# A first attention laid in written orders with its value product in two halves, and last sums moved into the last layer bodies

## The reference

```
xn  = layernorm(x)
out = x + attention(xn) + ffn(xn)
```

## Time and profile before

| | us |
|---|---|
| median of 3 runs | 3527.9 (3526.22 to 3528.53) |
| the profiled execution, whole | 3527.28 |
| its span, first to last instruction | 3525.5 |
| PE busy, share | 3293.5, 93% |
| DVE busy, share | 2843.1, 81% |
| ACT busy, share | 1832.3, 52% |
| POOL busy, share | 2640.0, 75% |

### The profile page before, as it was taken

One profiled execution on the slowest core, in us unless ns is written; L12 is line 12 of the kernel. 1 busy time (PEld: TensorE's weight loads), 2 busy tenths in 40 slices (PEclk: granted clock), 3 DMA queues, 4 the chain that ended last, 5 costly groups with the idle time before them and its releaser, 6 DMA issues. The chain is left out here.

```text
span 3525.5 us, 69882 instructions
## 1 busy us (share of the span) xinstructions
PE 3293.5 (93%) x26940; PEld 1611.1 (46%) x26940; DVE 2843.1 (81%) x3289; ACT 1832.3 (52%) x2692; POOL 2640.0 (75%) x1918
## 2 busy tenths in 40 slices
PE   5788876899999999999999999999999999999986
PEld 3222222454555545454545455555555454545443
DVE  5788846888888888888888888888888888888862
ACT  2477772454545454555555555555454545455532
POOL 3133206998888888888888888888888888888850
PEclk7799998999999999999999999999999999999998
DMA  6232214333333323333323333333333233333211
GB/s 209 73 63 48 47 37 113 79 73 73 71 86 79 80 71 72 83 71 82 78 71 79 79 81 77 73 73 85 83 74 79 68 78 78 83 77 71 71 46 49
DMA packets 178233, 270.01 MB, mean 77 GB/s; under 512 B 42481, under 2 KB 67185, under 8 KB 176241
## 3 DMA queue, kind: packets, MB, share of 16 engines
q1 hardware_dynamic: 174160, 251.10, 29.6%
q10 hardware_dynamic: 3744, 14.43, 1.1%
HBM read 44.49 MB, written 19.55 MB: 18 GB/s over the span
## 5 line engine op out<-in xcount | busy, mean ns | idle before, releaser
L1084 DVE SCALAR_TENSOR_TENSOR ly_prod<-ly_pj_ps,ly_few,ly_tables 128x1024 f32<-128x1024 f32 x768 | 964.6, 1272 | 190.1 <-ACT ly_sq L1216 165.5
L1216 ACT ACTIVATE ly_sq<-ly_pj_ps 128x512 f32<-128x512 f32 x768 | 451.0, 601 | 745.8 <-PE ly_pj_ps L918 702.7
L918 PE MATMUL ly_pj_ps<-ly_xs,ly_wqk 128*128 128x512 f32 x1536 | 796.1, 616 | 35.2 <-DVE ly_prod L1084 22.5
L999 PE MATMUL ly_to_ps<-ly_u,ly_mvo 128*128 128x512 f32 x1536 | 720.6, 598 | 0.1
L1325 POOL TENSOR_TENSOR ly_sq<-ly_sq 128x512 f32<-128x512 f32 x384 | 491.6, 1280 | 220.0 <-ACT ly_sq L1216 219.8
L1247 ACT COPY ly_u<-ly_pair_ps 128x1024 f32<-128x1024 f32 x384 | 378.7, 1013 | 240.6 <-PE ly_pair_ps L987 240.6
L1329 POOL TENSOR_TENSOR ly_sx<-ly_sx,ly_smax 128x1024 f32<-128x1024 f32 x192 | 366.2, 1907 | 145.3 <-DVE ly_smax L1124 145.3
L918 PEld LDWEIGHTS ly_pj_ps<-ly_xs,ly_wqk 128*128 128x128 f32 x1536 | 269.2, 191 | 426.4 <-issue 291.5
L999 PEld LDWEIGHTS ly_to_ps<-ly_u,ly_mvo 128*128 128x128 f32 x1536 | 277.1, 190 | 287.2 <-issue 287.2
L987 PE MATMUL ly_pair_ps<-ly_pt,ly_xt 32*128 32x512 f32 x3072 | 385.3, 615 | 19.9 <-ACT ly_u L1247 13.0
L967 PE MATMUL ly_pair_ps<-ly_kbd,ly_qp 128*32 128x128 f32 x12288 | 374.7, 276 | 22.2 <-DMA ly_kbd<-ly_kr 18.9
(11 more groups left out here) (113 smaller groups left out, 4317.5 us busy)
## 6 DMA issues: line engine op xcount, KB each, us to landing
ly_qp<-ly_qr SPq DMA_DIRECT2D x768, 128.0 KB, 2.3
ly_kbd<-ly_kr SPq DMA_DIRECT2D x1536, 64.0 KB, 2.0
ga_parts_dram<-ga_parts SPq DMA_DIRECT2D x16, 384.0 KB, 2.3
ga_qs<-ga_parts_dram SPq DMA_DIRECT2D x96, 64.0 KB
ga_ks<-ga_parts_dram SPq DMA_DIRECT2D x96, 64.0 KB
ly_wqk<-in_wqk SPq DMA_DIRECT2D x24, 256.0 KB, 4.0
ly_mvo<-mvo_dram SPq DMA_DIRECT2D x6, 1024.0 KB, 6.4
mvo_dram<-ga_pt ACTq DMA_DIRECT2D x4, 1024.0 KB, 4.0
```

The costliest lines, as they stand in the source:

```text
L918: pe.matmul(pj_ps[:, j % 2, :], wqk[:, g, j % TILES, :], xs[:, n % 2, WIN:], start=True, stop=True).then_inc(proj_ready.sem, 1)
L999: last = pe.matmul(to_ps[:], mvo[:, h, :], u[:, :, :, h, :].rearrange("p t c q -> p (t c) q"), start=(h == 0), stop=(h == LH - 1))
L1084: dve.scalar_tensor_tensor(prod[:, k], pj_ps[:, j % 2, :].unsqueeze(1).to_broadcast([P, 2, N]), gains[:, n // B, k:k + 1], tables[:, table ...
L1216: act.activation(sq[:, k, :], pj_ps[:, j % 2, :], ACT.Square).then_inc(sq_done.sem, 1)
```

## The change

- **Attention, orders.** The loops over quads are replaced by one written order per engine (`body(x_0, x_1, x_2, x_3)`, batches i, i-1, i-2, i-3). Score pairs are numbered 0 to 31 (`second(n, i)`), first pairs and maxima likewise. The first score pair of a batch and the first three exponentials are issued at the end of the body before, the last maximum and last product in the body after. `project` is issued by tile, four a batch.
- **Value product.** `pv` becomes `meet(n, q, half)`: 256 columns at a time, placed separately in the order. The same number of columns in all, twice the matmuls.
- **Folds.** A fold has four steps instead of three parts. Layers 0 to 3 write `s_ps` instead of `f_ps`, wait for `early_taken`, and have two buffers in `pt` in turn, `folded_1` and `gained` of their own. Layers 0 and 1 and most of layer 2 are folded in body 0, the rest of 2 and layer 3 in body 1. The tokens of batches 1 to 7 are turned together (`turn_others`) after step 9. Layer 4 begins in bodies 8 and 9; its last two steps and all of layer 5 (steps 18 to 23) are in body 10, behind the last product. The first exponential waits for the stores of layers 2 and 3.
- **SP's order.** Key parts are sent after the maxima of the batch before and stacked last.
- **End.** `final_part` is gone. `load_sums` loads the sums into `wqk` and `tables` when they are free; `turn_back` transposes X into `pj_ps`, for batches 0 and 1 at the end of body 51, 2 to 6 in body 52, 7 after it; `add_sums` adds into the same buffers and `store` writes them out.

The core of the diff:

```diff
-            def pv(b, q):
+            def meet(n, q, half):
...
+                lo = N // 2 * half
                 for c in range(4):
-                    last = pe.matmul(pv_ps[32 * c:32 * c + 32, :], va[:, b % 3, kt, 4 * j + c, :], pt[:, (QUADS * b + q) % 3, c, :],
-                                     start=(kt == 0), stop=(kt == T - 1), skip_group_check=True)
-                last.then_inc(pv_done.sem, 1)
+                    last = pe.matmul(pv_ps[32 * c:32 * c + 32, lo:lo + N // 2], va[:, n % 3, kt, 4 * j + c, :], pt[:, (QUADS * n + q) % 3, c, lo:lo + N // 2],
+                                     start=(kt == 0 and half == 0), stop=(kt == T - 1), skip_group_check=True)
+                if half:
+                    last.then_inc(pv_done.sem, 1)
...
+            def body(x_0, x_1, x_2, x_3):
+                project(x_0, 0); project(x_0, 1); second(x_2, 1); first(x_2, 31); meet(x_3, 15, 0); first(x_1, 0); second(x_2, 2)
+                meet(x_3, 15, 1); fold(x_3, 18); transposed_maxima(x_2, 1); second(x_2, 3); meet(x_2, 0, 0); fold(x_1, 11)
+                first(x_1, 1); project(x_0, 2); project(x_0, 3); second(x_2, 4); first(x_1, 2); fold(x_1, 12); meet(x_2, 0, 1)
+                fold(x_0, 0); out(x_3, 3); fold(x_3, 19); fold(x_3, 20); fold(x_3, 21); fold(x_3, 22); fold(x_3, 23); second(x_2, 5)
+                fold(x_0, 1); first(x_1, 3); second(x_2, 6); first(x_1, 4); meet(x_2, 1, 0); second(x_2, 7); values(x_0)
+                first(x_1, 5); meet(x_2, 1, 1); second(x_2, 8); first(x_1, 6); meet(x_2, 2, 0); second(x_2, 9); fold(x_0, 2)
...
+                first(x_1, 18); meet(x_2, 8, 1); transposed_maxima(x_1, 0); second(x_2, 21); fold(x_0, 8); first(x_1, 19)
+                fold(x_0, 9); turn_others(x_0); meet(x_2, 9, 0); second(x_2, 22); fold(x_0, 10); first(x_1, 20); meet(x_2, 9, 1)
...
+                first(x_1, 25); fold(x_2, 17); second(x_2, 28); first(x_1, 26); meet(x_2, 12, 0); meet(x_2, 12, 1); second(x_2, 29)
+                fold(x_1, 15); first(x_1, 27); meet(x_2, 13, 0); fold(x_1, 16); meet(x_2, 13, 1); second(x_2, 30); first(x_1, 28)
+                meet(x_2, 14, 0); second(x_2, 31); first(x_1, 29); meet(x_2, 14, 1); out(x_2, 2); second(x_1, 0); first(x_1, 30)
...
+            def body(x_0, x_1, x_2, x_3):     # ACT
+                exponentials(x_2, 3, 4); take(x_3, 3); exponentials(x_2, 5, 6, 7, 8, 9, 10, 11, 12, 13, 14, 15); gain_early(x_0, 0)
+                take_early(x_0, 0); take_early(x_0, 1); take_early(x_0, 2); gain_early(x_0, 1); pass_on(x_0, 0); take_early(x_0, 3)
+                take_early(x_0, 4); take_early(x_0, 5); take_early(x_0, 6); copy_values(x_0)
+                exponentials(x_2, 16, 17, 18, 19, 20, 21); pass_on(x_0, 1); take(x_2, 0)
...
+                take_early(x_0, 7); exponentials(x_2, 40); gain_early(x_0, 2); exponentials(x_2, 41, 42, 43, 44, 45, 46, 47)
+                copy_others(x_0); exponentials(x_2, 48); take_early(x_1, 11); exponentials(x_2, 49); take_early(x_0, 8)
...
+            def body(x_0, x_1, x_2, x_3):     # SP
+                send_maxima(x_2, 1); take_maxima(x_2, 1); send_parts(x_0, 0); stack(x_0, 0); send_maxima(x_1, 0); send_parts(x_0, 1)
+                take_maxima(x_1, 0); stack(x_0, 1); store_sum(x_2); store_late(x_2, 0); store_late(x_2, 1)
...
+            def turn_back(*items):
+                for b in items:
...
+                    if b >= 2:
+                        pe.wait_ge(res_done, b - 1)
+                    pe.wait_ge(x2_done.sem, x2_done.at(LAST + b, 1))
+                    for t in range(T):
+                        last = pe.transpose(pj_ps[:, b % 2, t * P:(t + 1) * P], X[:, b, 1 + t * P:1 + (t + 1) * P], ident[:])
+                    last.then_inc(res_ready, 1)
...
+            def add_sums(*items):
+                for b in items:
+                    dve.wait_ge(res_ready, b + 1)
+                    dve.wait_ge(sums_in[b // half], 16)
+                    dve.tensor_tensor(sums(b), pj_ps[:, b % 2, :], sums(b), ALU.add).then_inc(res_done, 1)
```

More of the change, by code:

```diff
@@ L87 @@
 GROUPS_LN = ((0, 1), (1, 4), (4, 8))
[L88 to L92, removed]
+OTHERS = range(1, B)
+EARLY = 4
 def global_attention_part(nc, x_dram, w_dram, rope_dram, ident_dram, X, sum_dram, parts_dram, maxes_dram, d):
@@ L189, in global_attention_part, with bodies, folds, fold_views @@
         where = {}
[L191 to L195, removed]
+        def bodies(body):
+            for i in range(B + 3):
+                body(*(known(i - k) for k in range(4)))
+        def folds(n, layer):
+            return n == (0 if layer < EARLY else B - 1)
+        def fold_views(layer, part):
+            k, f = layer % 2, s_ps[:, 0:2] if layer < EARLY else f_ps[:, where["fold", layer, part]]
             if part < 2:
-                return (folded_vo[late].rearrange("p (j h z c) -> p j z h c", j=2, z=2, c=P)[:, part],
-                        f_ps[:, k].rearrange("p z (h c) -> p z h c", c=P))
-            return folded_1[late], f_ps[:, k].rearrange("p z n -> p (z n)")[:, 0:F1]
+                return (folded_vo[layer].rearrange("p (j h z c) -> p j z h c", j=2, z=2, c=P)[:, part], f.rearrange("p z (h c) -> p z h c", c=P))
+            return folded_1[:, k], f.rearrange("p z n -> p (z n)")[:, 0:F1]
         @block.sync
@@ L361, in fold @@
                     pe.wait_ge(raw_loaded[k].sem, raw_loaded[k].at(layer // 2, 48))
-                to = slot(("fold", layer, part), taken, taken.at(at, part + 1))
+                if layer >= EARLY and part < 3:
+                    slot(("fold", layer, kind), late_taken, late_taken.at(layer - EARLY, kind + 1))
+                elif part < 3 and i:
+                    pe.wait_ge(early_taken.sem, 3 * layer + part)
+                f = s_ps[:, 0:2] if layer < EARLY else f_ps[:, where["fold", layer, kind]]
@@ L418, in _ @@
+            bodies(body)
         @block.vector
@@ L629, in _, with exponentials @@
-            stages(body)
+            def exponentials(n, *heads):
+                if n is None:
+                    return
+                for at in heads:
+                    quad = QUADS * n + at // 4
+                    if n == 0 and at == 0:
+                        for k in range(2):
+                            act.wait_ge(early_stored[k].sem, early_stored[k].at(EARLY // 2 - 1, 32))
+                    if quad >= 3 and at % 4 == 0:
+                        act.wait_ge(pv_done.sem, quad - 2)
+                    act.wait_ge(s_ready.sem, s_ready.at(n, at + 1))
+                    act.activation(pt[:, quad % 3, at % 4, :], s_ps[:, (64 * n + at) % 3, :], ACT.Exp, scale=float(GD) ** -0.5).then_inc(exp_done.sem, 1)
@@ L811, in layers_part @@
         where = {}
+        LAST = ITEMS - B
+        half = B // 2
+        sums = lambda b: wqk[:, b].rearrange("p t c -> p (t c)") if b < half else tables[:, b - half]
         def bodies(body):
@@ L884, in _ @@
             bodies(body)
+            load_sums()
+            for b in range(B):
+                store(b)
+            sp.wait_ge(res_stored, 16 * B)
         @block.tensor
```

607 lines of the change are left out of this document (286 added, 321 removed).

## The result

The changed kernel takes 3469.3 us (median of 4 runs, 3465.5 to 3471.9) against 3527.1 beside it: ratio 0.9834, interval 0.9821 to 0.9847. The profiled execution took 3465.5, its span 3463.4. I forecast 3460, within 3440 to 3487: the profiled execution is 5 us over it, the median 9.

The account below looks back on a forecast made before the run. No engine was full before, PE and ACT waiting in turn; after the change DVE was to bound steady bodies. Terms for bodies, tail and end sum to -67.2 us: 3527.3 to 3460 us, range 3440 to 3487.

Parts of the forecast that it names:

- The mechanism: Steady attention stages: PE and ACT wait for each other in turn, 2.67 us a quad; half products between score pairs end it.
- DVE sets the pace inside: Steady bodies: one more pair of maxima costs DVE 1.14 us, ACT 1.08, PE 1.04; DVE's sum is 41.5 us.
- 41.1 us: PE's summed work in a steady body: score pairs, products, shape switches, projections, output transposes, values and turned maxima.
- 60 cycles a matmul: Overhead rule weighed against halves: 3.2 us more PE a body, body near 47.5; the forecast took no such cost.
- Bodies 3 to 7, 8: Steady attention bodies 3 to 7: 44.3 us each, -35.9 together; body 8, without projections and values: 40.0 us, -6.2.
- Body 2: Attention body 2: 44.3 steady, plus 2.8 for low clock, plus 2.0 for a late store: 49.1 us, -5.2.
- Body 0: Start of the attention: token copies wait behind ACT's DMA issues; body 1 begins at about 59.6 us, -2.5.
- Body 1: Attention body 1: folds grow from 9.7 to 13 us of PE, partly hidden by maxima: change 0, from -4 to +4.
- Body 9, tail: Body 9, bounded by ACT alone: 36.5 us, -8.6; tail from last exponential to layers: 18.3 for 12.0, +6.3.
- End: Final part after the layers: 8.0 us for 23.1, -15.1, bounds -17 to -12.
- The last item's chain: Last layer bodies: turn_back(2) stands ahead of up(0) on PE and waits for add_sums(0), adding 1.4 us.
- SP's queue keeps its time: Attention: key parts go out behind the maxima, some 27 us into a body; 12 loads issued by about 38 of 44.

Follow-up runs that it names:

- the fillers' run: The changed kernel with one more unused 256-column matmul behind each of the 32 first score pairs of batch 0: 3468.7 us, ratio 0.9838.
- the folds moved: The changed kernel with fold steps 17 to 23 moved from behind the last exponential into the body of batch 7's exponentials: 3473.4 us, ratio 0.9848.

## Why the prediction was right or wrong

**The mechanism: right.** I said that PE and ACT wait for each other because 1.00 us of product stands ahead of the next scores, and that halves between pairs end it. Halves alone take the steady body from 51.5 to 47.5.

**"DVE sets the pace inside": wrong.** This is the step that failed, with the sum under it, "41.1 us" for PE, which is busy for 44.0. Taken from start to next start in the same body, the 22 halves that stand alone cost 0.57 each and the ten that stand in five adjacent pairs 1.00 a pair, 17.5 us where I had 16.0. The other terms are each within 0.6, and the sum comes to 42.6. Eight waits behind score pairs add the tails that busy time counts, 1.3, and 2.2 us of idle make the 46.0 up to 0.1. So the sum was 1.5 too low, in the term "16 products at 1.00 = 16". My sums had DVE ahead by only 0.4 (41.5 to 41.1), so that was enough to name the wrong engine.

The extra of the halves was undersized too: I had 1.6 us for the changes between shapes and nothing for the halves themselves, and the work rises by an estimated 2.8 from whole to half products in the same order. The earlier trace rows had a hint, PE busy 43.0 in the stage of before, above DVE's 42.6 and above my sum for more work, though a part of the 43.0 is tails ahead of waits. I built the sum from single rows and did not hold it against the busy time of the same stage.

By the Trainium skill's 60 cycles a matmul (TensorEngine Tiling, Instruction Overhead) the 128 added matmul records should have cost an estimated 3.2 us and the body 47.5. The runs show some 2.8 and 46.0, near the rule in sum but not in its form: two adjacent halves, 16 records, take the same 1.00 us as one whole product of 8, and the extra is at the halves that stand alone between score pairs. The rule did point to the right engine.

**Bodies 3 to 7, 8:** 46.4 us on average for 44.3, and 44.7 for 40.0. Body 8 repeats the error: I gave DVE's 38.9 plus a little, and it has 41.6 of DVE and 41.1 of PE.

**Body 2:** forecast 49.1, measured 50.8 and 49.4. The two causes I named, low clock and the wait for the store, are both there, but I added them as separate terms: with the wait taken apart it is 46.5, and the clock is 0.97.

**Body 0:** forecast start of body 1 at 59.6, measured 58.2 and 57.5, for the reason given (ACT's issues hold the token copies). **Body 1:** forecast unchanged, -10. I compared folds with folds and did not see that the clock of 0.53 in the one execution I had can be 0.63 with the same instructions. What gives the rest stays open.

**Body 9, tail: right.** 37.2 for 36.5; 18.8 for 18.3.

**End: the total right, one term not.** Behind the last `ffn_sum` pass 5.2 us for 6.6. The last item's chain was to grow by 1.4 us. From the end of `normalise` to the end of `ffn_sum` it went from 10.40 to 11.15, but the 10.40 has a stretch at the low level in it. Like with like: three executions with the old end take 10.24 to 10.40 at a clock of 0.84 to 0.86, three with the new end 12.53 to 12.63 at 0.86, so the chain grew by some 2.3 us (at full clock the new one takes 11.14 or 11.15, in six executions). Timeline of PE, before and after:

```profile
3492.02 6.98 PE L1016 MATMUL ly_pair_ps<-ly_xn,ly_w1c 128*128 128x512 f32 x12 [0.84 <-DVE ly_xn L1105]
```
```profile
3447.67 0.66 PE L1097 MATMUL ly_pj_ps<-ly_ident,x_all 128*128 128x128 f32 x4 [1.44 <-DVE ly_wqk L1244]
3448.16 1.88 PE L1078 MATMUL ly_pair_ps<-ly_xn,ly_w1c 128*128 128x512 f32 x4
```

`up` starts 0.05 us behind the end of `normalise` before (3491.97) and 1.15 behind it now (3447.01): this is the wait I priced, 1.1 for 1.4. What I left out are the transposes of batches 3, 4 and 5 between the parts of `up` and ahead of `down`, 0.43 each.

**"SP's queue keeps its time": half right.** It holds by a thin margin: in one execution bodies 3 and 5 were 0.6 and 1.1 longer, with waits for key parts in them, in the other none.

## What to carry to other kernels

Hold a bottom-up sum of an engine's work against its busy time in the same window before you name the bound; where two engines come out within a few us, change the work of each alone, as here, before you believe either. When two engines wait for each other, splitting the one long instruction group between them can pay more than it costs as long as the engine that splits has idle time to spend: here 4 us a body. In a kernel that swings by 5 us and more with its clock, judge an edit by the stretch it touches, compare stretches at the same granted clock, and don't judge one execution's stray wait at all.

## What the runs showed of the hardware

- TensorE's granted clock can fall to the low level with hardly any idle time, behind or within steps of one-column matmuls: at 101 us in the fillers' run, at 451 and 468 with the folds moved, PE busy 9.90 and 9.61 of 10 us around the last two. The narrow matmuls are what these falls have in common, but they are not enough: behind the same step at 60.53 in the changed kernel the clock stays at 1.00. The cause stays open.
- Four column groups of 128 x 256 float32 take 0.57 us alone between score pairs, two such sets one behind the other 1.00, and one of 128 x 512 1.00. A split in width costs 14% at most.
- A pair of 512 columns in bf16 takes 0.22 us to the next pair and 0.31 to a product in column groups.
- The same instructions take longer at a lower granted clock: the last item's chain 11.15 us at 1.00 and 12.53 to 12.63 at 0.86, bodies 1 and 2 of the attention of before together 103.4 us at 0.63 and 0.97 and 108.9 at 0.53 and 0.91.
- Layers and end took 2970.8 to 2980.7 us with the same instructions. The clock is part of that, not all: two executions with the same lost clock there, (1 - clock) x length of 21.2 and 21.3 us, took 2974.4 and 2977.7.
